# One fused attention and mixture-of-experts kernel: a new instruction order, a sigmoid from silu, and a router with stationary weights

## The chip, the cores and the metric

The kernel runs on one core of a Trainium2 chip, as one program that is launched once. The metric is the device time of one execution in microseconds (us). The engines are named as in the profile: PE (TensorE's matmuls) and PEld (its weight loads), DVE (VectorE), ACT (ScalarE), POOL (GpSimd) and SP (SyncE, which issues most DMAs).

## What is computed

The input x is 8 x 2048 rows of 256 numbers, all float32. A layer norm, linear attention and a residual come first; then a second layer norm, a mixture of experts with a router, a causal convolution of four taps along the sequence, and a second residual:

```python
x = x + attn(layernorm(x))          # Q, K, V of width 64; energy = K^T V over each sequence
x = x + ffn(layernorm(x))
# ffn, with h the normalized rows:
scores = sigmoid(h @ Wr)                       # 8 scores a row
idx = top_k(scores + router_bias, 2)           # two of them are kept
w = scores[idx] / (sum(scores[idx]) + 1e-9)    # cw: these weights, zero elsewhere
hid = silu(h @ Wg[e]) * (h @ Wu[e])            # four experts of width 128
out = sum_e cw[e] * (hid @ Wd[e]) + (cw[4] + cw[6]) * h + cw[7] * relu(h) + conv(h) + conv_b
```

## The kernel before, in words

The 16384 rows are cut into 32 groups of 512 (four tiles of 128 rows); four groups make one sequence. The work on a group is cut into stages, and the loop is a software pipeline: in one step each stage works on another group (`LAG`, line 34). The stages are L (statistics and first norm), A (its Gram matrix and transposes), Q (queries), B (attention, residual, second norm), R (transposes, router), C (the four experts and the convolution) and Y (last part of the experts, output). All steps are unrolled from step 7 to 39 (`steps`, line 319); the first seven are written out in `head()`. Once per sequence a chain of small matmuls turns the Gram matrix into the attention's map, in the step where B is on the first group of the sequence (`st.chain()`, line 91): the chain step, every fourth. `st.drain()` (line 94) is true at the end, when stage A has nothing left.

There is no planner in the code: each engine has a function `body(st)` that lists its part of one step in a fixed order, and semaphores hold an instruction until its input is there. An engine runs its list strictly in order, so that a waiting instruction holds back all behind it.

Products are made of float32r halves: of a number, `hi` is its rounded float32r copy and `lo` the rest, and a product is hi x hi + hi x lo + lo x hi (`three`, line 404). So each tile is copied by ACT to `hi` (for example `hid_high`, line 766), and then the rest is taken by DVE or POOL (`hid_low`, line 1014, `x2T_low`, line 1119, `xn_low`, line 1032, on DVE; `last_low`, line 1329, on POOL for the last expert).

TensorE's order in a step is `body` at line 687: `gate_up(0..7)` (two for each expert e, six matmuls of 512 columns each), `down` (12 matmuls of 256 columns an expert), `x2_transpose`, `router`, `conv_transpose`, the two halves of `attention`, `q_project`, `gram_halves`, `weights_transpose` and `xn_transpose`. `router` (line 537) uses the transposed rows x2T as stationary weights in float32 and 8 columns of Wr as the moving operand, eight matmuls that the profile shows as 16 instructions. `conv_transpose` adds the finished convolution into the experts' PSUM bank and so needs all taps of it.

DVE's order is at line 1225. `conv_tap` (line 1021) adds two of the six convolution taps, one for each half of the columns; `hidden` (line 1004) multiplies up by the weighted gate, `residual`, `norm1_stats` and `norm2_stats` serve the norms, `halo` (line 1162) copies six columns of the group before, and `route` (line 1074) finds the two largest scores and the weights `cw` in some 19 small instructions.

POOL's order is at line 1382: `gate_weight` (line 1322) multiplies an expert's gate by its row weight, 128x512; `power` (line 1366) takes e to the power of minus the logits and adds one, the denominator of the sigmoid; `norm1_factors`, `norm2_factors` and `skip_factors` are instructions on four columns; `relu_add` issues a DMA that adds.

ACT's order is at line 930: `silu` of the gates, the `hi` copies, `logits_copy` (line 865), the norms, `conv_begin`, and the two parts that take skip and relu into the sum.

The sigmoid of the kernel before and the instruction that divides:

```python
g.tensor_tensor(enx[:, :], inv_e[:, :], logits[:, :], ALU.pow)    # POOL, line 1368
g.tensor_tensor(den[:, :], enx[:, :], one_e[:, :], ALU.add)       # POOL, line 1372
v.reciprocal(flat(score[:, :, :]), den[:, :])                     # DVE, line 1088
```

## Time and profile before

| what | value |
|---|---|
| median of 3 runs | 894.48 us (891.71 to 897.38) |
| the profiled execution's own time | 893.6 us |
| its span, first to last instruction | 891.8 us |
| PE busy | 855.9 us, 96% |
| PEld busy | 754.3 us, 85% |
| DVE busy | 741.1 us, 83% |
| ACT busy | 628.7 us, 71% |
| POOL busy | 572.7 us, 64% |
| mean granted TensorE clock | 0.989 of 2.4 GHz |

The profile is of one execution; 1.8 us of its time lie outside the span. Shares are averages over the head, 27 full steps and the drain. Matmuls are pipelined: an instruction's duration overlaps the next one's, and the distance between two starts is what one costs. The same holds for DVE and ACT, where the next instruction's record begins some 0.1 us before the last one ends.

### The profile page before, as it was taken

To read this page: it belongs to the slowest core of one execution; us is meant where nothing else is said; L and a number is where in the kernel's file an instruction comes from. 1 tells how busy PE (TensorE), PEld (TensorE's weight loads), DVE (VectorE), ACT (ScalarE), POOL (GpSimd) and SP (SyncE) were. 2 spreads that over 40 slices of the span, in tenths; PEclk is the share of its full clock that TensorE was granted. 3 is DMA by queue.
4 is the path that set the end of the run, shared out by engine and by line. 5 is a ranking of instruction groups with operands and counts; after the bars stand their busy time and mean duration, and the time that the engine had idled before them with its cause. 6 is when DMAs were issued, how large, how long until landed. Compare 5 with 4: busy or idle time off the path is not lost.

```text
span 891.8 us, 16729 instructions
## 1 busy us (share of the span) xinstructions
PE 855.9 (96%) x5437; PEld 754.3 (85%) x5437; DVE 741.1 (83%) x2056; ACT 628.7 (71%) x1238; POOL 572.7 (64%) x654
## 2 busy tenths in 40 slices
PE   5789999999999999999999999999999999999997
PEld 4668989898888888988889888888888898788876
DVE  5758889988888998888898888899888887767775
ACT  5676777777687777778677777777777775655643
POOL 3336776667676657667666767666576766556663
PEclk9989999999999999999999999999999999999999
DMA  9111434543334543343544343454424344433333
GB/s 286 57 52 47 137 121 142 143 117 99 95 119 142 144 142 68 114 129 120 143 143 114 101 115 99 143 144 142 119 72 119 101 114 119 111 104 100 106 91 84
DMA packets 79446, 103.86 MB, mean 116 GB/s; under 512 B 6528, under 2 KB 58880, under 8 KB 79360
## 3 DMA queue, kind: packets, MB, share of 16 engines
q1 hardware_dynamic: 74752, 86.02, 30.4%
q0 software_dynamic: 4608, 16.78, 10.0%
q8 instruction: 43, 0.70, 0.3%
q14 instruction: 43, 0.35, 0.1%
HBM read 68.96 MB, written 17.04 MB: 96 GB/s over the span
## 4 chain that ended last, share of the span: by engine, by line
PE 66%; DVE 13%; POOL 12%; issue 5%; ACT 4%; DMA 0%; POOLq 0%; ACTq 0%; DVEq 0%
PE ps_gu L406 9%; PE ps_gu L408 9%; PE ps_gu L407 9%; POOL enx L1368 7%; PE ps_y L406 5%; PE ps_y L408 5%; PE ps_y L407 5%; PE ps_sh L543 4%; PE ps_sh L533 3%; POOL gate L1327 3%; PE ps_sh L516 2%; DVE stats L1065 2%; DVE acc L1057 2%; ACT x L840 2%; PE ps_y L456 2%
## 5 line engine op out<-in xcount | busy, mean ns | idle before, releaser
L1327 POOL TENSOR_TENSOR gate<-gate,cwb 128x512 f32<-128x512 f32 x128 | 167.5, 1309 | 127.8 <-ACT gate L763 126.4
L406 PE MATMUL ps_gu<-x2T_hi,wgu_hi 128*128 128x512 f32 x512 | 212.2, 414 | 0.0
L408 PE MATMUL ps_gu<-x2T_hi,wgu_lo 128*128 128x512 f32 x512 | 203.0, 396 | 0.0
L407 PE MATMUL ps_gu<-x2T_lo,wgu_hi 128*128 128x512 f32 x512 | 202.2, 395 | 0.0
L1368 POOL TENSOR_TENSOR enx<-inv_e,logits 128x32 f32<-128x32 f32 x32 | 177.5, 5546 | 8.6 <-ACT logits L756 8.6
L406 PE MATMUL ps_y<-wd_hi,hid_hi 128*128 128x256 f32 x512 | 152.8, 299 | 4.0 <-DVE hid_lo L1018 3.1
L1029 DVE SCALAR_TENSOR_TENSOR conv<-x2T,conv_w,conv 128x512 f32<-128x512 f32 x192 | 146.4, 801 | 0.0
L408 PE MATMUL ps_y<-wd_hi,hid_lo 128*128 128x256 f32 x512 | 145.3, 284 | 0.0
L407 PE MATMUL ps_y<-wd_lo,hid_hi 128*128 128x256 f32 x512 | 144.2, 282 | 0.0
L1011 DVE TENSOR_TENSOR hid<-ps_gu,gate 128x512 f32<-128x512 f32 x128 | 86.0, 672 | 39.2 <-POOL gate L1327 38.1
L408 PEld LDWEIGHTS ps_gu<-x2T_hi,wgu_lo 128*128 128x128 f32 x512 | 96.9, 189 | 22.5
L406 PEld LDWEIGHTS ps_gu<-x2T_hi,wgu_hi 128*128 128x128 f32 x512 | 97.6, 191 | 19.2 <-DVE hid L1011 3.0
L407 PEld LDWEIGHTS ps_gu<-x2T_lo,wgu_hi 128*128 128x128 f32 x512 | 97.4, 190 | 13.4
L406 PEld LDWEIGHTS ps_y<-wd_hi,hid_hi 128*128 128x128 f32 x512 | 98.5, 192 | 6.7 <-DVE hid_lo L1018 4.3
L763 ACT ACTIVATE gate<-ps_gu 128x512 f32<-128x512 f32 x128 | 75.3, 588 | 40.6 <-PE ps_gu L408 39.0
L1018 DVE TENSOR_TENSOR hid_lo<-hid,hid_hi 128x512 fp32r<-128x512 f32 x96 | 68.8, 716 | 41.6 <-ACT hid_hi L756 41.6
L756 ACT ACTIVATE hid_hi<-hid 128x512 fp32r<-128x512 f32 x128 | 80.2, 626 | 32.1 <-DVE hid L1011 31.5
L407 PEld LDWEIGHTS ps_y<-wd_lo,hid_hi 128*128 128x128 f32 x512 | 97.4, 190 | 1.6
L1306 POOL TENSOR_TENSOR mv<-mv,eps_ln 128x4 f32<-128x4 f32 x64 | 13.5, 211 | 132.2 <-DVE mv L1068 112.8
L408 PEld LDWEIGHTS ps_y<-wd_hi,hid_lo 128*128 128x128 f32 x512 | 97.1, 190 | 0.0
L840 ACT ACTIVATE x<-acc,shift,rstd 128x256 f32<-128x256 f32 x128 | 66.5, 591 | 8.8 <-POOL shift L1311 8.2
L824 ACT ACTIVATE xn<-xa,shift,rstd 128x256 f32<-128x256 f32 x128 | 66.0, 589 | 8.2 <-POOL shift L1311 8.1
(115 smaller groups left out, 1934.3 us busy)
## 6 DMA issues: line engine op xcount, KB each, us to landing
cwb<-cw_rows SPq DMA_DIRECT2D x128, 256.0 KB, 4.0
xa<-in_x SPq DMA_DIRECT2D x32, 512.0 KB, 7.5
acc<-in_x SPq DMA_DIRECT2D x32, 512.0 KB, 6.7
acc<-x POOLq DMA_DIRECT2D x32, 512.0 KB, 4.6
out<-acc SPq DMA_DIRECT2D x64, 256.0 KB, 2.3
cwb<-in_wg SPq DMA_DIRECT2D x4, 128.0 KB, 4.0
cwb<-in_wu SPq DMA_DIRECT2D x4, 128.0 KB, 3.8
cwb<-in_wd SPq DMA_DIRECT2D x1, 512.0 KB, 4.5
```

What stands on the lines that cost most here:

```text
L406: nc.tensor.matmul(dst, a_hi, b_hi, start=start, stop=False, skip_group_check=True)
L407: nc.tensor.matmul(dst, a_hi, b_lo, start=False, stop=False, skip_group_check=True)
L408: return nc.tensor.matmul(dst, a_lo, b_hi, start=False, stop=stop, skip_group_check=True)
L756: return nc.scalar.activation(dst, src, ACT.Copy, scale=scale)
L763: nc.scalar.activation(gate[:, e % 2], ps_gu[GU_BANK[2 * e]][:, :], ACT.Silu)\
L824: nc.scalar.activation(xn[:, q, t], xa[:, q, t], ACT.Identity, bias=shift1[:, f, t:t + 1], scale=rstd1[:, f, t:t + 1]).then_inc(xn_ready, 1)
L840: nc.scalar.activation(x2[:, q, t], acc[:, st.slot("B", 4), t], ACT.Identity, bias=shift2[:, q, t:t + 1], scale=rstd2[:, q, t:t + 1]).then ...
L1011: v.tensor_tensor(hid[:, e % 2], ps_gu[GU_BANK[2 * e + 1]][:, :], gate[:, e % 2], ALU.mult)\
L1018: v.tensor_tensor(hid_lo[:, k], hid[:, k], hid_hi[:, k].bitcast(F32), ALU.subtract)\
L1029: v.scalar_tensor_tensor(conv[:, c], x2T[:, q, c, k:k + GT], conv_w[:, c, k:k + 1], conv[:, c], ALU.mult, ALU.add).then_inc(conv_ready, 1)
L1327: g.tensor_tensor(gate[:, e % 2], gate[:, e % 2], cwb[:, q, e], ALU.mult).then_inc(gatew_ready, 1)
L1368: g.tensor_tensor(enx[:, :], inv_e[:, :], logits[:, :], ALU.pow).then_inc(enx_ready, 1)
```

## The change

On TensorE the router becomes four passes of 512 columns: `wr2` holds the hi half of Wr in columns 0 to 7, the lo half in 8 to 15 and zeros beyond, stays as weights, and the hi and lo halves of x2T move through. The result lies transposed, 16 rows by 512; ACT copies it (`logitsT_copy`), and behind the fourth gate-up `logits_rows` transposes it back, four times 16x128. ACT copies the rows (`parts_copy`), and POOL adds the two halves (`logits_sum`).

The sigmoid is made of silu: ACT takes the absolute value (`logits_size`), DVE bounds it from below (`magnitude`), ACT takes silu of its negative (`score_dip`); at the head of `route` DVE divides by the size, adds one where the logit is positive, and takes the larger of the result and its negative. `power` goes.

`xn_low` and the `lo` halves of experts 1 and 2 go from DVE to POOL (`xn_low`, `gate_low`). The order of the four engines changes as the diff shows. Left out of the diff are declarations, the head's and the weights' small additions, and the constants.

```diff
             def router(st):
-                pe.wait_ge(x2T_ready, st.before("R", HC, HC))
+                if st.before("R") == 0:
+                    pe.wait_ge(wrlo_out, 1)
+                b, q = ps_sh[0], st.slot("R", 2)
                 pe.wait_ge(x2Tlo_ready, st.before("R", HC, 1))
-                b, q = ps_sh[0], st.slot("R", 2)
+                pe.wait_ge(x2Thi_ready, st.before("R", HC, HC))
+                for c in range(HC):
+                    nc.tensor.matmul(b[:, :], wr2[:, c], x2T_hi[:, q, c], start=(c == 0), stop=False,
+                                     skip_group_check=True)
+                for c in range(HC):
+                    if c == 1:
+                        pe.wait_ge(x2Tlo_ready, st.before("R", HC, HC))
+                    last = nc.tensor.matmul(b[:, :], wr2[:, c], x2T_lo[:, q, c], start=False, stop=(c == HC - 1),
+                                            skip_group_check=True)
+                last.then_inc(router_done, 1)
+
+            def logits_rows(st):
+                pe.wait_ge(logitsT_ready, st.before("R", 1, 1))
                 for t in range(TG):
-                    for c in range(HC):
-                        last = nc.tensor.matmul(b[:, t * NE:(t + 1) * NE],
-                                                x2T[:, q, c, PAD + t * P:PAD + (t + 1) * P], wr_sb[:, c],
-                                                start=(c == 0), stop=(c == HC - 1))
-                last.then_inc(router_done, 1)
+                    last = nc.tensor.transpose(ps_sh[0][:, t * 2 * NE:(t + 1) * 2 * NE],
+                                               logitsT[0:2 * NE, t * P:(t + 1) * P], ident[0:2 * NE, 0:2 * NE])
+                last.then_inc(rows_done, 1)
...
@@ -711,24 +734,22 @@
                     pe.wait_ge(et_out, st.chains(2, 2))
                 if c_on:
                     gate_up(st, 3)
+                if r_on:
+                    logits_rows(st)
                 if m_on:
                     chain_f(st)
-                if b_on and drain:
+                elif b_on:
                     attention(st, 0)
                 if c_on:
                     gate_up(st, 4)
-                if b_on and drain:
+                if b_on and not m_on:
                     attention(st, 1)
                 if c_on:
+                    gate_up(st, 5)
                     conv_transpose(st)
                     down(st, "C", 0)
-                if b_on and not m_on and not drain:
-                    attention(st, 0)
-                if c_on:
-                    gate_up(st, 5)
                 if m_on:
                     attention(st, 0)
-                if b_on and not drain:
                     attention(st, 1)
                 if c_on:
                     gate_up(st, 6)
...
-            def logits_copy(st):
+            def logitsT_copy(st):
                 act.wait_ge(router_done, st.before("R", 1, 1))
-
+                copy(logitsT[:, :], ps_sh[0][0:2 * NE, :]).then_inc(logitsT_ready, 1)
+
+            def parts_copy(st):
+                act.wait_ge(rows_done, st.before("R", 1, 1))
                 if st.later("R", 1):
-                    act.wait_ge(enx_ready, st.before("R"))
-                copy(logits[:, :], ps_sh[0][:, 0:TG * NE]).then_inc(logits_ready, 1)
+                    act.wait_ge(logits_ready, st.before("R"))
+                copy(parts[:, :, :], ps_sh[0][:, 0:TG * 2 * NE].rearrange("p (t n) -> p t n", t=TG))\
+                    .then_inc(parts_ready, 1)
+
+            def logits_size(st):
+                act.wait_ge(logits_ready, st.before("R", 1, 1))
+                nc.scalar.activation(size[:, :], logits[:, :], ACT.Abs).then_inc(size_ready, 1)
+
+            def score_dip(st):
+
+                act.wait_ge(mag_ready, st.before("R", 1, 1))
+                if st.later("R", 1):
+                    act.wait_ge(cw_ready, st.before("R"))
+                nc.scalar.activation(dip[:, :], mag[:, :], ACT.Silu, scale=-1.0).then_inc(dip_ready, 1)
...
             def body(st):
                 c_on, r_on, m_on = st.on("C"), st.on("R"), st.chain()
                 if m_on:
                     gram_copy(st)
                 if c_on:
                     silu(st, 0)
+                if st.on("A"):
+                    xn_split(st)
                 if r_on:
                     x2T_out(st, 0)
                 if m_on:
                     gramT_copy(st)
+                elif c_on:
+                    hid_high(st, 0)
                 if r_on:
                     x2T_out(st, 1)
                 if m_on:
@@ -945,27 +1005,26 @@
                     silu(st, 1)
                 if m_on:
                     et_copy(st)
-                if r_on:
-                    logits_copy(st)
+                    hid_high(st, 0)
+                if r_on:
+                    logitsT_copy(st)
+                if c_on and not m_on:
+                    relu_part(st)
+                if r_on:
+                    parts_copy(st)
                 if m_on:
                     f_copy(st)
-                if c_on:
-                    hid_high(st, 0)
-                if st.on("A"):
-                    xn_split(st)
+                    relu_part(st)
+                if c_on:
+                    hid_high(st, 1)
+                if r_on:
+                    logits_size(st)
                 if c_on:
                     silu(st, 2)
-                    hid_high(st, 1)
-
-                    q = st.slot("C", 2)
-                    act.wait_ge(skip_ready, st.before("C", 2, 2))
-                    for t in range(TG):
-                        a = acc[:, st.slot("C", 4), t]
-                        nc.scalar.activation(a, a, ACT.Identity, bias=skip_bias[:, q, t:t + 1],
-                                             scale=skip_scale[:, q, t:t + 1]).then_inc(ident_added, 1)
-                    for t in range(TG):
-                        nc.scalar.activation(x2[:, q, t], x2[:, q, t], ACT.Relu, scale=cw[:, q, EM + 3, t:t + 1])\
-                            .then_inc(relu_ready, 1)
+                if r_on:
+                    score_dip(st)
+                if c_on:
+                    skip_part(st)
                 if r_on:
                     conv_begin(st)
                 if c_on:
@@ -973,10 +1032,10 @@
                     hid_high(st, 2)
                 if st.on("L"):
                     norm1(st)
+                if st.on("B") and not m_on:
+                    norm2(st)
                 if r_on:
                     weights_copy(st)
-                if st.on("B") and st.drain():
-                    norm2(st)
                 if st.on("Q"):
                     q_high(st)
                 if st.on("A") and r_on:
@@ -985,7 +1044,7 @@
                     hid_high(st, 3)
                 if st.on("A") and r_on:
                     xnT_high(st, 1)
-                if st.on("B") and not st.drain():
+                if m_on:
                     norm2(st)
...
-            def xn_low(st):
-                dve.wait_ge(xnhi_ready, halved(st, 1))
-
-                dve.wait_ge(gram_done, st.before("A"))
-                v.tensor_tensor(xn_lo, xn[:, st.slot("A", 4)], xn_hi.bitcast(F32), ALU.subtract)\
-                    .then_inc(xnlo_ready, 1)
...
+            def magnitude(st):
+                dve.wait_ge(size_ready, st.before("R", 1, 1))
+                if st.later("R", 1):
+                    dve.wait_ge(dip_ready, st.before("R"))
+                v.tensor_scalar(mag[:, :], size[:, :], LEAST, None, ALU.max).then_inc(mag_ready, 1)
...
-                dve.wait_ge(den_ready, st.before("R", 1, 1))
-                done(v.reciprocal(flat(score[:, :, :]), den[:, :]))
+                dve.wait_ge(mag_ready, st.before("R", 1, 1))
+                done(v.reciprocal(rmag[:, :], mag[:, :]))
+                dve.wait_ge(dip_ready, st.before("R", 1, 1))
+                after()
+                done(v.tensor_tensor(minor[:, :], dip[:, :], rmag[:, :], ALU.mult))
+                after()
+                done(v.scalar_tensor_tensor(signed[:, :], logits[:, :], 0.0, minor[:, :], ALU.is_gt, ALU.add))
+                after()
+                done(v.scalar_tensor_tensor(flat(score[:, :, :]), signed[:, :], -1.0, signed[:, :], ALU.mult, ALU.max))
...
@@ -1229,43 +1298,37 @@
                 if c_on:
                     dve.wait_ge(halo_ready, st.before("C", 1, 1))
                     conv_tap(st, 0)
+                    hidden(st, 0)
+                if r_on:
+                    x2T_low(st, 0)
+                if c_on:
+                    conv_tap(st, 1)
+                if r_on:
+                    x2T_low(st, 1)
                 if st.on("L"):
                     norm1_stats(st)
-                if r_on:
-                    x2T_low(st, 0)
-                if c_on:
-                    conv_tap(st, 1)
-                if r_on:
-                    x2T_low(st, 1)
+                if c_on:
+                    hid_low(st, 0)
+                if c_on:
+                    hidden(st, 1)
                 if y_on:
                     output(st, 0)
                     output(st, 1)
-                if c_on:
-                    hidden(st, 0)
+                if r_on:
+                    magnitude(st)
+                if c_on:
                     conv_tap(st, 2)
-                    hid_low(st, 0)
-                    hidden(st, 1)
-
                 if m_on:
                     f_low(st)
-                drain = st.drain()
-                if c_on:
-                    hid_low(st, 1)
-                if st.on("A"):
-                    xn_low(st)
-                if b_on and drain:
+                elif b_on:
                     residual(st, 0)
                     residual(st, 1)
                     norm2_stats(st)
-                if r_on and c_on and not b_on:
+                if c_on:
+                    hidden(st, 2)
+                if r_on:
                     route(st)
-                if c_on:
-                    hidden(st, 2)
-                if r_on and c_on and b_on:
-                    route(st)
-                if c_on:
-                    hid_low(st, 2)
-                if b_on and not drain:
+                if m_on:
                     residual(st, 0)
                     residual(st, 1)
                     norm2_stats(st)
...
+            def gate_low(st, e):
+
+                pool.wait_ge(hidhi_ready, st.before("C", EM, e + 1))
+                k = e % 2
+                g.tensor_tensor(hid_lo[:, k], hid[:, k], hid_hi[:, k].bitcast(F32), ALU.subtract)\
+                    .then_inc(hidlo_ready[k], 1)
+
+            def xn_low(st):
+                pool.wait_ge(xnhi_ready, halved(st, 1))
+                g.tensor_tensor(xn_lo, xn[:, st.slot("A", 4)], xn_hi.bitcast(F32), ALU.subtract)\
+                    .then_inc(xnlo_ready, 1)
...
-            def power(st):
-                pool.wait_ge(logits_ready, st.before("R", 1, 1))
-                g.tensor_tensor(enx[:, :], inv_e[:, :], logits[:, :], ALU.pow).then_inc(enx_ready, 1)
-                pool.wait_ge(enx_ready, st.before("R", 1, 1))
+            def logits_sum(st):
+                pool.wait_ge(parts_ready, st.before("R", 1, 1))
                 if st.later("R", 1):
-                    pool.wait_ge(rt, st.before("R", RT, 1 - RT))
-                g.tensor_tensor(den[:, :], enx[:, :], one_e[:, :], ALU.add).then_inc(den_ready, 1)
+                    pool.wait_ge(cw_ready, st.before("R"))
+                    pool.wait_ge(size_ready, st.before("R"))
+                g.tensor_tensor(logits[:, :].rearrange("p (t e) -> p t e", t=TG), parts[:, :, 0:NE],
+                                parts[:, :, NE:2 * NE], ALU.add).then_inc(logits_ready, 1)
...
             def body(st):
-                c_on, r_on = st.on("C"), st.on("R")
+                c_on, r_on, b_on, m_on = st.on("C"), st.on("R"), st.on("B"), st.chain()
                 if c_on:
                     gate_weight(st, 0)
+                if st.on("A"):
+                    xn_low(st)
+                if c_on:
                     gate_weight(st, 1)
-                if r_on:
-                    power(st)
-                if c_on:
+                norm1_factors(st)
+                if r_on:
+                    logits_sum(st)
+                if c_on:
+                    gate_low(st, 1)
                     gate_weight(st, 2)
-                    norm1_factors(st)
-                    if st.drain():
-                        relu_add(st)
-                        if st.on("B"):
-                            norm2_factors(st)
+                if b_on and not m_on:
+                    norm2_factors(st)
+                if c_on:
+                    gate_low(st, 2)
                     gate_weight(st, 3)
-                if c_on and not st.drain():
                     relu_add(st)
-                if st.on("B") and not st.drain():
+                if m_on:
                     norm2_factors(st)
                 if c_on:
-                    last_low(st)
+                    gate_low(st, 3)
                 if r_on:
                     skip_factors(st)
```

## Rows read from the trace of the kernel before

**Rows 1.** Busy us by stretch: PE, PEld, DVE, ACT, POOL (instructions); clock, DMA share, GB/s.
```profile
167.21:192.50 25.29, 25.29 (x168) 22.61 (x166) 22.67 (x65) 19.19 (x39) 17.63 (x21) 1.00 0.44 126
...
217.90:246.60 28.70, 28.66 (x189) 24.87 (x187) 24.23 (x66) 20.97 (x46) 18.71 (x21) 1.00 0.40 111
...
sum 104.79, PE 104.64 PEld 92.81 DVE 92.64 ACT 78.65 POOL 71.85; mean PE 26.16 PEld 23.20 DVE 23.16 ACT 19.66 POOL 17.96
```

**Rows 2.** Timeline of PE in an ordinary step: start, us, engine, line, operation, shape, count.
```profile
167.21 0.48 PE L406 MATMUL ps_gu<-x2T_hi,wgu_hi 128*128 128x512 f32 x1
...
172.06 0.60 PE L533 MATMUL ps_sh<-ident,x 128*128 128x128 f32 x4
172.41 0.48 PE L406 MATMUL ps_gu<-x2T_hi,wgu_hi 128*128 128x512 f32 x1
172.73 0.39 PE L407 MATMUL ps_gu<-x2T_lo,wgu_hi 128*128 128x512 f32 x1
...
173.89 1.85 PE L543 MATMUL ps_sh<-wr_sb,x2T 128*128 128x8 f32 x16
175.59 0.47 PE L406 MATMUL ps_gu<-x2T_hi,wgu_hi 128*128 128x512 f32 x1
```

**Rows 3.** Timeline of DVE, four stretches.
```profile
67.74 2.41 DVE L1029 SCALAR_TENSOR_TENSOR conv<-x2T,conv_w,conv 128x512 f32<-128x512 f32 x2
...
122.96 2.26 DVE L1029 SCALAR_TENSOR_TENSOR conv<-x2T,conv_w,conv 128x512 f32<-128x512 f32 x2
...
168.87 0.71 DVE L1172 COPY x2T<-x2T 128x6 f32<-128x6 f32 x1
169.49 1.42 DVE L1029 SCALAR_TENSOR_TENSOR conv<-x2T,conv_w,conv 128x512 f32<-128x512 f32 x2
170.83 1.40 DVE L1046 BATCH_NORM_STATS2 stats<-xa 128x6 f32<-128x256 f32 x4
...
172.62 0.65 DVE L1122 TENSOR_TENSOR x2T_lo<-ps_sh,x2T_hi 128x512 fp32r<-128x512 f32 x1
...
180.81 1.22 DVE L1036 TENSOR_TENSOR xnT<-xn,xnT 128x1024 fp32r<-128x1024 f32 x1
...
186.04 1.08 DVE L1101 SCALAR_TENSOR_TENSOR raw<-marked,score 128x32 f32<-128x32 f32 x1
```

**Rows 4.** Timeline of POOL in the same stretches.
```profile
67.73 1.87 POOL L1327 TENSOR_TENSOR gate<-gate,cwb 128x512 f32<-128x512 f32 x1 [1.12 <-ACT gate L763]
...
122.74 1.27 POOL L1327 TENSOR_TENSOR gate<-gate,cwb 128x512 f32<-128x512 f32 x1 [3.88 <-ACT gate L763]
...
168.25 1.30 POOL L1332 TENSOR_TENSOR hid_lo<-hid,hid_hi 128x512 fp32r<-128x512 f32 x1
...
171.07 1.29 POOL L1327 TENSOR_TENSOR gate<-gate,cwb 128x512 f32<-128x512 f32 x1
...
176.06 5.44 POOL L1368 TENSOR_TENSOR enx<-inv_e,logits 128x32 f32<-128x32 f32 x1
...
185.78 1.30 POOL L1327 TENSOR_TENSOR gate<-gate,cwb 128x512 f32<-128x512 f32 x1 [0.69 <-ACT gate L763]
```

**Rows 5.** Timeline of ACT just ahead of an ordinary step.
```profile
167.12 0.62 ACT L756 ACTIVATE hid_hi<-hid 128x512 fp32r<-128x512 f32 x1
```

**Rows 6.** Groups of POOL: line, operation, shapes, count, busy us, mean ns, idle before.
```profile
L1368 POOL TENSOR_TENSOR enx<-inv_e,logits 128x32 f32<-128x32 f32 x32 | 177.5, 5546 | 8.6 <-ACT logits L756 8.6
L1327 POOL TENSOR_TENSOR gate<-gate,cwb 128x512 f32<-128x512 f32 x128 | 167.5, 1309 | 127.8 <-ACT gate L763 126.4 <-DMA cwb<-cw_rows 1.4
...
L1306 POOL TENSOR_TENSOR mv<-mv,eps_ln 128x4 f32<-128x4 f32 x64 | 13.5, 211 | 132.2 <-DVE mv L1068 112.8 <-DVE mv L1049 18.6 <-ACT xn L824 0.8
```

**Rows 7.** Groups of ACT, the same columns.
```profile
L967 ACT ACTIVATE x<-x,cw 128x256 f32<-128x256 f32 x128 | 54.2, 495 | 0.0
...
L763 ACT ACT_TABLE_LOAD x1 | 1.3, 1283 | 0.0
```

**Rows 8.** Waits of PE's weight loads: total us, times, longest us.
```profile
PEld ps_sh L606 <- DVE cw L1115: 6.0, 4, 1.8
```

74 lines of the change are left out of this document (51 added, 23 removed).

## The prediction

> **What bounds the kernel now.** I first read the busy time by stretch, cut where a step's first gate-up matmul starts [rows 1]. An ordinary step (167.21 to 192.50) takes 25.3 us and TensorE is busy in all of it at full clock; every fourth, the chain step, takes 28.7 with 28.66 busy. DVE has 22.7 of 25.3, ACT 19.2, POOL 17.6. So a step is TensorE's instructions laid end to end, and one of another engine costs nothing until a matmul waits for it. Second, TensorE's order within one step [rows 2]: which matmul starts when tells how late each input may be. Third, DVE and POOL side by side [rows 3, 4]: where the small slack of the others goes. Four steps take 104.8 us; the loop has 27 full steps (7 of them chain steps) and a drain of six.
>
> **The pair of engines that cannot overlap.** At 122.74 a POOL product (1.27 us) begins; the two convolution taps that DVE starts at 122.96 take 2.26 instead of the 1.42 of the pair at 169.49. At 186.04 a 128x32 instruction of DVE takes 1.08 and ends 0.04 after the POOL product of 185.78; at 168.87 a copy of six columns takes 0.71 and ends with POOL's hid_lo. The other way round: at 67.73 the taps were first, and POOL's product took 1.87. DVE instructions with one input in SBUF (batch statistics at 170.83 beside POOL's product of 171.07: 1.40 for four, 0.41 each) run beside POOL undisturbed, and so does xn_low beside the long pow, at 180.81 beside 176.06: pow is long but does not hold what DVE needs [rows 3, 4]. So a large POOL instruction and a DVE instruction with two SBUF inputs exclude each other: the later one waits for the other's end, a tap then ends some 0.55 after it, and in the pair of taps POOL gets its turn between them. The change takes the harmless 5.4 us of pow off POOL and puts four excluding instructions there.
>
> **The parts, and their cost.**
> *Router.* Out go 16 instructions from 173.89 to 175.59, 1.70, plus the longer first pitch behind small matmuls, 0.08 (172.41 to 172.73 is 0.32, not 0.23): 1.78. In come four passes of 512 columns at 0.23 (the five matmuls from 172.73 to 173.89): 0.92. The four row transposes, with 16 rows and 16 moving columns, are not in the trace. The nearest row is the four 128x128 transposes, 0.35 at 172.06 plus 0.08 behind: 0.11 each, and the router's sixteen come to 0.11 each too, which is the upper end; below, 16 moving columns instead of 128 could make them nearly free, 0.03 each. I take the nearest row, 0.11, so 0.43 together. Gain 1.78 - 0.92 - 0.43 = 0.43 a step, up to 0.74. "TensorE: Matmul & The Clock Gate" (the Trainium skill, LDWEIGHTS) says that a weight load costs by its columns (number / 1.2 in ns) and not by its rows. By that rule 128 columns are 0.107 and the four transposes 0.43, an estimate, where the lower bound would make them 0.12; no row here shows a load of 16 rows.
> *Sigmoid.* POOL loses pow, 5.5 a step [rows 6], and a small addition; ACT gains two small activations, a rows copy and a 16x512 copy instead of a small one, about 1.1; DVE gains magnitude, minor, signed and a max, about 0.2 each. All of it is off TensorE's path as long as its users are not late: rows wait for the copy of the transposed logits (0.2 after the router, 0.6 long, against 1.39 of gate-up cover), the second attention half for the rows copy (cover 1.9).
> *xn_low to POOL.* DVE loses 1.22. On POOL a 128x1024 subtraction is not in the trace: at least the 1.31 of the 128x512 product, at most twice it, 2.62. From 0.21 at 4 elements and 1.31 at 512 a line gives 2.4; I take that [rows 6].
> *hid_low 1 and 2 to POOL.* DVE loses 2 x 0.6, POOL gains 2 x 1.3. POOL's excluding work goes from 5 x 1.3 to 7 x 1.3 + 2.4 = 11.5 of 25 us.
> *Order.* attention halves, the convolution transposes and ACT's and POOL's parts move; what counts is who is late now. DMA issues stay in their queues.
>
> **First wait, in an ordinary step.** Times from the start of gate-up 0 (167.21), by hand from the rows. ACT's hid_high 3 starts 0.09 before it and takes 0.62 [rows 5], so POOL's gate_low 3 runs 0.57 to 1.86, the halo copy ends with it and the skip factors alternate with conv tap 0. Gate product 0 came 2.82 after that hid_lo (168.25 to 171.07), so 3.39 to 4.68. Only then comes hidden 0 (4.72 to 5.39) and x2T_low 0 (to 5.99). xn_low has the pair from 4.64 to 7.03; conv tap 1, asking at 5.92, ends 7.58 and 8.25 instead of 6.66 and 7.34; x2T_low 1 ends 8.84. The router's fourth pass needs it. In TensorE's order the router starts at 6.68 and this pass at 7.37: wait 1.5. Before, the router needed no second half of x2T_lo. Behind xn_low on POOL stands gate product 1, which hidden 1 has not asked for yet. Bounds: with xn_low at 1.3 the taps run unhindered, x2T_low 1 ends 7.94 and the wait is 0.6; at 2.62 it is 1.7.
>
> **Second wait.** Router done 9.1; then gate-up 3, rows, attention 0, gate-up 4, attention 1, gate-up 5: the convolution transposes are due at 14.64. DVE after x2T_low 1: statistics 1.8 (170.83 to 172.62), hid_low 0.6, hidden 1 0.6 (11.8), two outputs 1.2: 13.0, then magnitude. But hidden 1 lets ACT copy (to 12.49) and POOL start gate_low 1, 12.5 to 13.8. Magnitude waits until 13.85; gate product 2, its gate ready at 13.6, is in front of conv tap 2 until 15.0; the taps end at 15.55 and 16.2. Wait 1.6. If the taps come first, the product falls between them and the end is the same to 0.1; with both taps ahead of it, about 0.6. Ordinary step: 25.3 - 0.43 + 1.5 + 1.6 = 28.0.
>
> **Chain step.** The router is later behind the chain matmuls, so the first wait is gone. But magnitude stands ahead of conv tap 2 on DVE and waits for ACT's logits_size, which now stands behind f_copy (from 12.1, 0.7), four relu parts (0.5 each, 0.1 of it beneath the next, [rows 7]) and hid_high 1: 15.2. By then gate_low 1 holds the pair to 16.4 and gate product 2 to 17.6; taps end 18.8; transposes due at 14.9: wait 3.9. 28.7 - 0.43 + 3.9 = 32.2. Behind it norm2 stands at ACT's end as before, and x2's first transposes wait 0.3: 28.4. Route, norm2 statistics, gate_low 2 and weights end over 0.7 before their users in both.
>
> **Sum.** Four steps 2 x 28.0 + 32.2 + 28.4 = 116.6 against 104.8: +11.8. 26 full steps (the last has no xn_low) are 6.5 of these: +77. Head and drain, where TensorE is not the bound and pow goes but the exclusion stays: 0, between -8 and +5. The profiled execution took 893.6 (span 891.8), 0.9 under the median of the runs, 894.48: 893.6 + 77 = about **970**.
>
> **Rivals.**
> *The gain arrives whole* (faster; place: POOL's meetings with DVE). pow, 5.5 us, stands between the logits and the weights of every group, and in the drain the transposes of the weights wait up to 1.8 for them [rows 6, 8]. If POOL's new products fall beside DVE instructions that read PSUM or one operand, as nearly all do now (the pair of taps at 169.49 is undisturbed), no wait is added: 0.43 in each of 31 steps with a router is 13, and 1.7 in six drain steps about 10: 893.6 - 23 = **870**. More it cannot be in the full steps: a chain step has 0.04 of TensorE idle. Against it: by the walk above POOL takes the pair while taps 1 and 2 are next on DVE. It decides where the added waits average under 0.43 a step.
> *DVE gets its turn whenever it asks.* For it: at 67.73 taps that began 0.01 after the product were served first. Against it: 122.96, 168.87, 186.04 and some 25 like it. Then x2T_low 1 ends near 7.8 (wait 0.45, step 25.3), the second wait vanishes, the chain step still waits 1.75 for logits_size (30.0): four steps 105.9, 26 of them +7, the drain -10: **891**.
> *Half of it collides*: xn_low takes 1.3 and both taps of conv 2 come ahead of gate product 2. Waits 0.6 and 0.6, steps 26.1, 31.2 and 26.4: four 109.8, +33, **927**: same side, smaller.
> *Activation tables swap.* If Abs and Silu were in different tables, each step would load twice, 1.28 each [rows 7]; before, there are two loads in the whole run. logits_size, then silu 2 come 1.3 later, and with them the second wait: +1.3 x 26 on the forecast, **1004**. "ScalarE: Activation LUTs" (the Trainium skill, Table sets) says that cheap functions, abs among them, are in every set; by that this cannot happen. No row has Abs, so I keep a small chance.
>
> **How the numbers follow.** Forecast 0.72, with its own range 935 to 1000; half collision 0.09; gain whole 0.10; DVE first 0.05; tables 0.04. A change of 1% (885.5 to 903.4) is about what a measurement of this kernel tells from none: DVE first lies within it, with 0.01 of the whole gain; a little of it goes below. So faster 0.11, same 0.06, slower 0.83. Range 890 to 1003: the whole gain, half of DVE first and the tables stay outside.
>
> **What would show it.** Right: ordinary steps of about 28 us; a TensorE gap of 1 to 2 us ahead of the router's last pass, released by DVE's x2T_lo, and one ahead of the convolution transposes, released by conv; taps of 1.3 to 1.8 us beside POOL's xn_low and gate; POOL's xn_low near 2.4; sixteen router instructions of 1.7 us replaced by 0.9 + 0.43. Wrong: TensorE still without gaps and a step under 25.3; taps all at 0.74; POOL products of 1.8 us instead, which would be DVE first; table loads in every step.

## The result, and the profile after

The changed kernel takes 1121.5 us (median of 4 runs, 1119.8 to 1124.9), the kernel before 894.6 in the same comparison: ratio 1.254, interval 1.250 to 1.257. The forecast was 970, its range 890 to 1003. The side was right; the size was short by 151 us. The profiled execution spans 1121.1 us.

The table of stretches, the full steps and then the drain, first of after, then of before; the columns are those of [rows 1].

```profile
58.96:934.16 875.20, 731.80 (x4204) 618.40 (x4203) 618.57 (x1692) 535.33 (x1084) 451.61 (x567) 0.93 0.33 92
934.16:1121.10 186.94, 146.65 (x780) 120.26 (x778) 108.97 (x274) 85.49 (x180) 75.65 (x94) 0.91 0.29 82
```

```profile
56.88:742.17 685.29, 680.41 (x4413) 603.26 (x4411) 601.06 (x1664) 511.45 (x1006) 463.23 (x514) 1.00 0.41 118
742.17:891.80 149.63, 136.10 (x820) 117.19 (x818) 104.74 (x266) 82.61 (x168) 88.25 (x89) 0.98 0.36 103
```

Of the 229 us between the spans, 190 came in the 27 full steps, 37 in the drain, 2 in the head (58.96 instead of 56.88). In the steps TensorE was busy in 680 of 685 us; now it is in 732 of 875, and the granted clock fell from 1.00 to 0.93. So PE has gaps, and no other engine is busy for a larger share of the steps than before: the time is in waits. One ordinary step, the chain step, and the sum of four steps (from 300.35 on):

```profile
333.05:365.84 32.79, 27.97 (x159) 23.55 (x158) 23.11 (x66) 20.04 (x41) 17.19 (x22) 0.92 0.34 97
...
398.73:433.58 34.85, 31.15 (x181) 26.61 (x179) 24.65 (x67) 21.23 (x46) 17.36 (x22) 0.90 0.32 92
sum 133.23, PE 113.67 PEld 96.09 DVE 93.98 ACT 82.50 POOL 70.01; mean PE 28.42 PEld 24.02 DVE 23.49 ACT 20.63 POOL 17.50
```

The steps were forecast at 28.0, 32.2 (chain) and 28.4 (behind it), 116.6 for four; they are 133.2. The waits of after (engine, tile, line waited for: us in total, times, longest), PE's and one of ACT's:

```profile
PE ps_y L467 <- DVE conv L1088: 64.0, 30, 5.0
PE ps_sh L527 <- ACT cwT L777: 63.1, 20, 3.8
PE ps_sh L555 <- ACT x2T_hi L777: 23.0, 15, 3.2
PE ps_sh L560 <- DVE x2T_lo L1187: 12.2, 16, 0.8
...
ACT x L863 <- issue: 129.9, 23, 7.8
```

Lines 467 and 560 are the two waits that were forecast, the convolution transposes and the router's last passes; line 555 is the router's first passes. Line 527, the second half of xn's transposes, waits for ACT's copy of the weights; nothing of it was in the forecast. And ACT itself stands 5.6 us in each of 23 steps (129.9 / 23) ahead of line 863, norm2, "issue", that is, for nothing that the profile names. The timeline of one ordinary step shows for what (start, us, engine, line, [idle before]):

```profile
358.31 0.92 POOL L1408 DMA_DIRECT2D acc<-x  x1
...
362.94 2.07 ACT L863 ACTIVATE x<-acc,shift,rstd 128x256 f32<-128x256 f32 x4 [5.22 <-issue]
364.92 0.25 ACT L777 ACTIVATE cwT<-ps_sh 16x128 f32<-16x128 f32 x1
...
365.31 0.88 PE L527 MATMUL ps_sh<-ident,xn 128*128 128x128 f32 x4 [3.09 <-ACT cwT L777]
...
333.63 0.63 PE L418 MATMUL ps_gu<-x2T_lo,wgu_hi 128*128 128x512 f32 x1
334.05 0.63 PE L419 MATMUL ps_gu<-x2T_hi,wgu_lo 128*128 128x512 f32 x1
```

The stretch from there on, its granted clock the last but two, and the DMA in the list of issues (KB each, us from issue to landing):

```profile
333.63:337.89 4.26, 4.26 (x11) 3.29 (x10) 2.90 (x5) 2.85 (x5) 3.27 (x6) 0.50 0.62 206
```

```profile
acc<-x POOLq DMA_DIRECT2D x32, 512.0 KB, 4.6
```

POOL issues `relu_add`'s accumulating DMA at 358.31. It lands 4.6 us later, at 362.9; norm2 starts at 362.94. In the steps on either side it is the same: issued at 325.24 and 391.33, norm2 at 329.94 and 395.98. norm2 writes x2, in two buffers; the one that it needs is the one this DMA is still reading, that of the group two before. The wait is in the code, `act.wait_ge(relu_added[...])` in `norm2`, and it was there before. What the change did is to move norm2 ahead of the weights copy in ordinary steps, so that the copy and all behind it on ACT stand behind the DMA. Then TensorE, after more than 3 us without work, starts the next step late and at nearly twice the distance from matmul to matmul: 0.42 us (333.63 to 334.05) instead of 0.23 [rows 2], with a granted clock of 0.50, the lower of its levels (1.2 of 2.4 GHz), until 337.89. In the kernel before, the DMA and norm2 of the step of 167.21:

```profile
187.03 0.92 POOL L1340 DMA_DIRECT2D acc<-x  x1
...
193.73 2.08 ACT L840 ACTIVATE x<-acc,shift,rstd 128x256 f32<-128x256 f32 x4 [0.18 <-POOL shift L1311]
```

With the same 4.6 us the DMA landed at 191.6, before ACT came to norm2, its last part, at 193.7.

The two forecast waits, in the steps from 300.35 and 333.05:

```profile
305.96 2.37 POOL L1400 TENSOR_TENSOR xnT<-xn,xnT 128x1024 fp32r<-128x1024 f32 x1
...
307.24 2.30 DVE L1088 SCALAR_TENSOR_TENSOR conv<-x2T,conv_w,conv 128x512 f32<-128x512 f32 x2
...
309.46 0.68 DVE L1187 TENSOR_TENSOR x2T_lo<-ps_sh,x2T_hi 128x512 fp32r<-128x512 f32 x1
...
310.19 0.51 PE L560 MATMUL ps_sh<-x2T_lo,wr 128*128 128x512 f32 x1 [0.75 <-DVE x2T_lo L1187]
...
346.89 1.29 POOL L1395 TENSOR_TENSOR hid_lo<-hid,hid_hi 128x512 fp32r<-128x512 f32 x1
...
347.23 0.99 DVE L1130 TENSOR_SCALAR mag<-size 128x32 f32<-128x32 f32 x1 [0.32 <-ACT size L901]
...
348.13 1.29 POOL L1389 TENSOR_TENSOR gate<-gate,cwb 128x512 f32<-128x512 f32 x1
348.13 2.50 DVE L1088 SCALAR_TENSOR_TENSOR conv<-x2T,conv_w,conv 128x512 f32<-128x512 f32 x2
350.69 0.55 PE L467 MATMUL ps_y<-ident,conv 128*128 128x128 f32 x3 [1.74 <-DVE conv L1088]
```

They are as forecast: taps 1 wait for the end of xn_low (308.33) and take 2.30, x2T_low 1 comes behind them; magnitude ends with gate_low 1 (348.2), taps 2 with 1.1 us under gate product 2. Three groups of after: xn_low takes 2.38 (2.4 was taken), magnitude 1.02 on average, and of the two table loads in the whole run one stands at the first silu of the scores, so nothing swaps in the steps.

```profile
L1400 POOL TENSOR_TENSOR xnT<-xn,xnT 128x1024 fp32r<-128x1024 f32 x26 | 61.9, 2382 | 0.0
L1130 DVE TENSOR_SCALAR mag<-size 128x32 f32<-128x32 f32 x32 | 32.6, 1020 | 22.1 <-ACT size L901 22.1
...
L908 ACT ACT_TABLE_LOAD x1 | 1.3, 1283 | 0.0
```

### The profile page after: what moved, and what is told of

The parts are those of the page before. It is cut to its first block and busy times, and to the rows that moved or that the text cites. A ratio compares the mean times of both kernels' runs of the same rounds, so it can differ in the third digit from the quotient of the medians.

```text
span 1121.1 us, 16479 instructions
## 1 busy us (share of the span) xinstructions
PE 918.0 (82%) x5181; PEld 771.5 (69%) x5181; DVE 763.1 (68%) x2095; ACT 657.7 (59%) x1335; POOL 543.6 (48%) x711
## 5 line engine op out<-in xcount | busy, mean ns | idle before, releaser
L1395 POOL TENSOR_TENSOR hid_lo<-hid,hid_hi 128x512 fp32r<-128x512 f32 x96 | 123.9, 1290 | 306.7 <-ACT hid_hi L777 306.7
L417 PE MATMUL ps_gu<-x2T_hi,wgu_hi 128*128 128x512 f32 x512 | 223.5, 436 | 0.4 <-DVE hid L1070 0.4
L418 PE MATMUL ps_gu<-x2T_lo,wgu_hi 128*128 128x512 f32 x512 | 216.0, 422 | 0.0
L419 PE MATMUL ps_gu<-x2T_hi,wgu_lo 128*128 128x512 f32 x512 | 214.9, 420 | 0.0
L1088 DVE SCALAR_TENSOR_TENSOR conv<-x2T,conv_w,conv 128x512 f32<-128x512 f32 x192 | 188.2, 1019 | 0.0
L863 ACT ACTIVATE x<-acc,shift,rstd 128x256 f32<-128x256 f32 x128 | 66.4, 590 | 135.5 <-issue 129.9
L419 PEld LDWEIGHTS ps_gu<-x2T_hi,wgu_lo 128*128 128x128 f32 x512 | 105.4, 206 | 25.6
L417 PEld LDWEIGHTS ps_gu<-x2T_hi,wgu_hi 128*128 128x128 f32 x512 | 106.5, 208 | 19.3 <-DVE hid L1070 3.1
L1200 DVE TENSOR_TENSOR q<-ps_gu,q 64x512 fp32r<-64x512 f32 x32 | 21.8, 682 | 135.0 <-ACT q L777 135.0
L527 PE MATMUL ps_sh<-ident,xn 128*128 128x128 f32 x256 | 45.4, 313 | 76.0 <-ACT cwT L777 63.1
L1368 POOL TENSOR_TENSOR mv<-mv,eps_ln 128x4 f32<-128x4 f32 x64 | 22.9, 358 | 141.6 <-DVE mv L1120 98.8
```

Source lines behind the costliest of these rows:

```text
L417: nc.tensor.matmul(dst, a_hi, b_hi, start=start, stop=False, skip_group_check=True)
L418: nc.tensor.matmul(dst, a_hi, b_lo, start=False, stop=False, skip_group_check=True)
L419: return nc.tensor.matmul(dst, a_lo, b_hi, start=False, stop=stop, skip_group_check=True)
L527: last = nc.tensor.transpose(ps_sh[c][:, t * P:(t + 1) * P], xn[:, st.slot("A", 4), t, c * P:(c + 1) * P], ident[:, :])
L863: nc.scalar.activation(x2[:, q, t], acc[:, st.slot("B", 4), t], ACT.Identity, bias=shift2[:, q, t:t + 1], scale=rstd2[:, q, t:t + 1]).then ...
L1088: v.scalar_tensor_tensor(conv[:, c], x2T[:, q, c, k:k + GT], conv_w[:, c, k:k + 1], conv[:, c], ALU.mult, ALU.add).then_inc(conv_ready, 1)
```

## The experiments

Each is one run beside the kernel before (890 to 897 us); e14 and e15 have three more rounds. "Four steps" is the sum of one chain step and three ordinary ones.

**1. norm2 back at ACT's end** (e1), as before, outside the drain; in the drain it stays where the change put it.

```diff
-                if st.on("B") and not m_on:
+                if st.on("B") and st.drain():
                     norm2(st)
...
-                if m_on:
+                if st.on("B") and not st.drain():
                     norm2(st)
```

> Theory A (norm2, moved ahead of the weights copy on ACT, waits for the DMA of relu_add; the second half of xn's transposes then comes 3.3 us late and the matmuls behind it run at half clock, together 5.9 us in three of four steps): with norm2 back at ACT's end four steps fall from 133.2 to about 115.5 and the time to 990-1020. Theory B (POOL and DVE excluding each other is the whole of it, norm2's wait only stands beside it): the step stays near 33 us, time above 1100.

1046.9 us, four steps 122.4. The wait of line 527 for the weights copy is gone, theory B falls. The gain is less than theory A gave (990 to 1020). norm2, 2 us at ACT's end, now stands ahead of the next step's copies of x2T, and line 555 waits 38.1 us for x2T_hi in all, where it was 23.0; that this is the whole difference was not shown. The drain is as long as in the changed kernel, 186.9.

**2. The DMA earlier, norm2 where the change put it** (e2).

```diff
                     gate_low(st, 1)
                     gate_weight(st, 2)
+                    relu_add(st)
...
                     gate_weight(st, 3)
-                    relu_add(st)
```

> norm2 keeps its new place, but its DMA is issued ahead of gate_low 2 and gate product 3 and lands before norm2 asks. Theory A: as with norm2 at the end, four steps about 115.5, and the drain gains too: 980-1015. Theory B: above 1100. Theory C (norm2 ahead of the weights copy is late by its own factors and 2 us long, the DMA has no part in it): 1060 or more.

1005.2 us: one line moved on POOL is worth 116 us, 97.8 in the full steps (777.4 instead of 875.2) and 19.6 in the drain (167.3 instead of 186.9). An ordinary step and the chain step behind it, and lines of the first's timeline:

```profile
332.85:361.38 28.53, 25.53 (x160) 21.71 (x159) 24.01 (x65) 20.21 (x42) 17.76 (x22) 1.00 0.38 111
361.38:395.46 34.08, 30.38 (x181) 26.34 (x179) 23.75 (x66) 20.16 (x45) 17.26 (x22) 0.90 0.34 94
```

```profile
349.70 0.93 POOL L1408 DMA_DIRECT2D acc<-x  x1 [1.31 <-ACT acc L976]
...
354.63 2.07 ACT L847 ACTIVATE xn<-xa,shift,rstd 128x256 f32<-128x256 f32 x4
356.60 2.07 ACT L863 ACTIVATE x<-acc,shift,rstd 128x256 f32<-128x256 f32 x4
359.36 0.27 ACT L777 ACTIVATE cwT<-ps_sh 16x128 f32<-16x128 f32 x1 [0.69 <-PE ps_sh L629]
```

The DMA is issued 6.9 us ahead of norm2, which follows norm1 without a gap, and the copy waits for nothing but its transposes. Theory A holds, though four steps take 119.8 and not its 115.5; theory C falls, since the copy no longer waits for norm2 once norm2's buffer is free. And the steps that are left, 28.5, 34.1 and 28.7 (395.46 to 424.15), come near the forecast ones: 28.0, 32.2 and 28.4.

**3. Gap or clock** (e12). In the changed kernel, 13 matmuls that nobody reads fill the gap ahead of line 527, the wait kept.

```diff
+                    if c_on and b_on and not m_on:
+                        pe.wait_ge(gate_ready, st.before("C", EM, EM))
+                        for _ in range(13):
+                            nc.tensor.matmul(ps_gu[GU_BANK[0]][:, :], wgu_hi[:, 0, 0, 0], x2T_hi[:, st.slot("C", 2), 0],
+                                             start=True, stop=True)
                     xn_transpose(st, 1)
```

> The changed kernel itself (1121.5 us), with 13 extra matmuls of 512 columns (3.0 us, their result is overwritten) in the gap ahead of the second half of xn's transposes, in the steps in which norm2 stands early. The wait stays. If a gap costs its length and then a clock at half speed behind it (12 matmuls at 0.43 instead of 0.23 us): the pitch behind stays 0.23 and four steps fall by about 4.5, time near 1090. If the matmuls behind the gap are slow for another reason: still 0.43, 1121 or more. If the next waits of the step end no sooner anyway: pitch 0.23, but 1115-1121.

```profile
363.56 0.63 PE L527 MATMUL ps_sh<-ident,xn 128*128 128x128 f32 x4
...
364.26 0.39 PE L418 MATMUL ps_gu<-x2T_lo,wgu_hi 128*128 128x512 f32 x1
364.49 0.40 PE L419 MATMUL ps_gu<-x2T_hi,wgu_lo 128*128 128x512 f32 x1
```

```profile
PE ps_sh L555 <- ACT x2T_hi L782: 42.9, 24, 3.2
```

The distance behind the filled gap is 0.23, so the idle time did lower the clock; yet the time is 1123.0, within what the changed kernel itself took (1119.8 to 1124.9), so the third branch. What the matmuls gained waits again one line on: line 555 for x2T_hi 42.9 us in all (23.0 without filling). The next step is late on ACT, and TensorE's half speed stood beside that. The 116 us are the held-up ACT, not the clock behind this gap.

**4. POOL's long products cut short** (e7), the order of e2 kept; parts of the two lo halves are left out.

```diff
-                g.tensor_tensor(hid_lo[:, k], hid[:, k], hid_hi[:, k].bitcast(F32), ALU.subtract)\
+                n = 16 if e == 1 and st.later("C", 2) else GT
+                g.tensor_tensor(hid_lo[:, k, 0:n], hid[:, k, 0:n], hid_hi[:, k, 0:n].bitcast(F32), ALU.subtract)\
...
-                g.tensor_tensor(xn_lo, xn[:, st.slot("A", 4)], xn_hi.bitcast(F32), ALU.subtract)\
+                g.tensor_tensor(xn_lo[:, 0:1, 0:16], xn[:, st.slot("A", 4), 0:1, 0:16],
+                                xn_hi[:, 0:1, 0:16].bitcast(F32), ALU.subtract)\
```

> The order of e2 untouched; POOL's xn_low takes 16 columns instead of 1024 and gate_low 1 takes 16 instead of 512, so the rest of both lo halves is left out of the result. If POOL's long products hold DVE's taps: taps 1 run at 0.74, the router's wait falls from 0.9 to 0.3 or less, the wait of the convolution transposes from 2.1 to about 1 (gate product 2 still meets a tap), four steps about 114, 965-985 us. If DVE's and ACT's order alone makes the waits: 1000-1006.

950.2 us, better than expected; four steps take 112.5. Line 560 no longer waits, line 467 waits 37.8 in all instead of 67.3. So shortening them is worth 55 of the 111 us that e2 is over the kernel before. How much of that is the exclusion and how much POOL's own shorter list, the run doesn't part, except at line 560, where xn_low can act through DVE alone. Line 555 still waits 20.4 us for x2T_hi (18.7 in e2), which the forecast did not have: the change put hid_high 0, which waits for DVE's hidden 0, ahead of x2T_out 1 on ACT. In e13 (experiment 8), where among other moves it stands behind, this wait is 1.8 us. The chain step is still 32.1; most of its wait is another, for ACT's logits_size.

**5. Tap 2 ahead of magnitude** (e9), on e2.

```diff
-                if r_on:
-                    magnitude(st)
                 if c_on:
                     conv_tap(st, 2)
+                if r_on:
+                    magnitude(st)
```

> e2 (1005.2 us) with conv tap 2 ahead of magnitude on DVE and nothing else. If what holds the convolution transposes is magnitude, which waits for logits_sum behind norm1_factors on POOL, and in the chain step for ACT's logits_size: the chain step's wait falls from 5 to about 1 us, the ordinary one's from 2.1 to 1 (one tap still meets gate_low 1), four steps from 119.0 to 111-113, 955-970 us. If the taps meet POOL's products whichever comes first: 990 or more.

953.0 us, four steps 108.6, the chain step 27.8 instead of 34.1 and so under the 28.7 of the kernel before. The convolution transposes wait 12.0 us in all instead of 67.3. What POOL's products delay here is small as long as tap 2 does not stand behind magnitude. Experiments 4 and 5 act on the same wait, so their gains can't simply be added; no run has both.

The 6.3 us of the chain step are more than its wait. In e2:

```profile
380.43 1.97 PE L467 MATMUL ps_y<-ident,conv 128*128 128x128 f32 x8 [3.66 <-DVE conv L1088]
382.05 0.56 PE L417 MATMUL ps_y<-wd_hi,hid_hi 128*128 128x256 f32 x1
```

```profile
382.05:384.75 2.70, 2.70 (x14) 2.70 (x13) 2.39 (x22) 1.52 (x2) 0.00 (x0) 0.50 0.97 184
387.48:388.90 1.42, 1.42 (x13) 1.42 (x12) 1.39 (x9) 1.23 (x3) 0.02 (x1) 1.00 0.00 0
```

The matmul before starts at 376.37, so the wait, less one distance of 0.23, is 3.8. Behind it the granted clock is 0.50: the twelve matmuls of down 0 take 2.70, those of down 1, at 1.00, 1.42. From 380.43 to the next gate-up at 386.08 TensorE takes 5.65, where the same work takes 3.3 in the one full chain step of e2 that kept its clock (from 500.13). So the wait and 2.3 us of half clock make nearly all of the 6.3. In five of the six full chain steps with this wait the clock costs 1.5 to 2.3 us, some 9 us together.

**6. xn_low on DVE again** (e3), on e2, behind hidden 0.

```diff
                     hidden(st, 0)
+                if st.on("A"):
+                    xn_low(st)
...
-                if st.on("A"):
-                    xn_low(st)
```

> As the run before, with xn_low back on DVE, behind hidden 0. If what is left after the norm2 wait is the exclusion between DVE and POOL, as the prediction had it, the router's wait (up to 1.5 us a step) goes and the time is 30-40 us under the run before. If xn_low's place has no part in what is left: within 10 us of the run before.

1039.3 us, 34 worse: a miss. Now x2T_low stands 1.2 us behind xn_low on DVE, the taps 1 are under gate product 1 instead of xn_low (the pair still takes 2.44 in the step from 344.99, where e2 has 2.33), and line 560 waits 39.8 instead of 14.9. The exclusion takes the next product that comes.

**7. x2T_low 1 ahead of tap 1** (e5), on e2, and tap 2 ahead of hid_low 0 as well (e6).

> relu_add early as in e2 (1005.2 us, four steps 119.0), and on DVE both x2T_low ahead of conv tap 1. If the router's wait comes from x2T_low 1 standing behind taps that POOL's xn_low holds up: that wait (0.9 us in three of four steps, with what the clock loses behind it) goes, four steps about 116, 980-990 us. If the wait ahead of the convolution transposes takes it back (its chain through norm1_factors and logits_sum on POOL does not start earlier): within 5 us of 1005.

> As e5, and conv tap 2 ahead of hid_low 0 and hidden 1, so that it no longer stands behind magnitude. If magnitude and POOL's gate_low 1 and gate product 2 make the second wait: it goes in all steps (2.1 in ordinary ones, 5 in chain steps), four steps 104-107, and 11 us of the drain: 900-930. If the exclusion only moves (the taps meet gate product 1 instead, hidden 1 and what follows it come later): 960 or more.

e5: 1074.0 us, worse by 69, against all that was expected. The router's wait for x2T_lo is gone, but DVE stands 1.07 us for x2T_hi 1, both taps then meet gate product 1, norm1's statistics come later, POOL's norm1_factors behind them, logits_sum behind these, and so magnitude and tap 2: line 467 waits 117.3 us in all. That chain through POOL is a part of the second wait which the forecast did not have; no run moved it alone. e6: 961.5, the chain step 27.8, but line 467 still waits in ordinary steps (28.0 to 28.4), now for the outputs that stand behind tap 2 (DVE's acc: 36.6 us in 21 steps).

**8. The waits taken out one after the other** (e13, e14, e15), on e9. Below is e13 on DVE; norm1_factors on POOL goes behind gate product 2, and in ordinary steps hid_high 0 on ACT behind x2T_out 1. e14 puts x2T_low 1 ahead of the two outputs, e15 moves route and norm2 in the drain:

```diff
+                if y_on:
+                    output(st, 0)
+                    output(st, 1)
                 if r_on:
                     x2T_low(st, 1)
                 if c_on:
                     conv_tap(st, 1)
-                if st.on("L"):
-                    norm1_stats(st)
...
+                    conv_tap(st, 2)
+                    hid_low(st, 0)
+                    hidden(st, 1)
+                if st.on("L"):
+                    norm1_stats(st)
```

> e9 (953.0 us, four steps 108.6) with what then is left taken out: on DVE both outputs between the two x2T_low, taps 1 and 2 together behind them and the statistics of norm1 behind hidden 1; on ACT hid_high 0 behind x2T_out 1; on POOL logits_sum ahead of norm1_factors. If the router's two waits (0.9 us each in ordinary steps) are all that is left: four steps 104-105.5, 923-935 us. If DVE itself, with 23 to 24 us of work a step and the exclusion on top, sets the step by then: 107 or more, 945 or more.

> e13 (918.2 us, four steps 106.2) with both x2T_low side by side and the outputs behind them. What is left in its ordinary steps is one wait of the router's fourth pass, 0.95 us, for x2T_low 1 behind the two outputs. If that is the last one: ordinary steps 25.1-25.3, four steps 103.2-104, 898-905 us, so the full steps are then at or under the 104.8 of the kernel before. If the outputs, now later, push taps 1 and 2 past the convolution transposes: 912 or more.

> As e14, and in the drain route ahead of norm2's statistics on DVE, norm2_factors behind gate product 3 on POOL, norm2 behind the weights copy on ACT. If the drain's loss (some 9 us over the kernel before) is the weights' transposes waiting up to 2.8 us for route, and the weights copy waiting behind norm2: 3 to 8 us less than e14, 892-900. If norm2, then later, makes the next x2 transposes wait instead: within 2 us of e14.

e13: 918.2 us, four steps 106.2, the steps longer than expected and the whole shorter. e14: 920.5 (ratio 1.030, 1.026 to 1.035), a miss: the router's last wait is gone, and another has come in its place, at the transposes of the weights (e13: 6.5 us, 4 times).

```profile
PE ps_sh L629 <- DVE cw L1180: 29.9, 24, 3.5
```

Four steps take 106.0, as with e13. The wait has moved along DVE's list from an early user to its last one, route. That points to DVE's list, with what holds it, as what sets the step by then; no run showed it by itself. e15: 925.5 (ratio 1.035, 1.027 to 1.043); the drain's rest was not the late route, or norm2 took it back; it stays open.

**9. The new parts in the old order** (e4; e8 and e10 move x2T_low 1 ahead; e11 the drain). Router, sigmoid and their helpers, with the order of the kernel before on all engines, xn_low and hid_low 1 and 2 on DVE; magnitude behind hid_low 1, score_dip behind the relu parts (e8 has both ahead).

> The new router and the new sigmoid alone, everything else in the order of the kernel before (halves of hid and xn on DVE again). By the prediction's own terms: 0.43 to 0.74 in each of 31 steps and about 10 in the drain, 865-885. If one of the new parts costs by itself (the transposes of 16 rows, a clock drop behind them, the two waits that rows and their copies add), 895 or more.

> As e4 (913.6 us: new router and sigmoid in the old order), with x2T_low 1 ahead of conv tap 1, magnitude ahead of hid_low 1 and score_dip ahead of the skip and relu parts. If what cost there was the router's fourth pass waiting for x2T_low 1 (0.5 to 0.7 a step) and the weights' transposes in the drain waiting 1.5 longer for the longer chain of the new sigmoid: 888-897 us. If the new parts cost by themselves: 908 or more.

> e4 (913.6 us, four steps 105.4) with x2T_low 1 between the two halves of conv tap 1 instead of behind both: 0.66 us earlier, and no new wait, since its input is there by then. If the router's fourth pass waits for it by 0.5 to 0.6 in ordinary steps: four steps 103.3-103.9, 899-904 us. If the e8 run's loss (an earlier x2T_low pushes tap 1 under POOL's gate product) comes here too: 920 or more.

> As e10, and in the drain alone magnitude ahead of hid_low 1, score_dip ahead of skip and relu, route ahead of norm2's statistics and hidden 2. If the drain's 11 us over the kernel before are the weights' transposes waiting for a route that stands late on DVE: 2 to 2.5 us less in four of its steps, 889-895 us. If norm2, then later, takes it back: within 2 us of e10.

e4: 913.6 us, against 865 to 885 if the parts had paid as forecast. e8, both x2T_low ahead of conv tap 1: 951.7, a miss of e5's kind (tap 1 under gate product 1; line 417 waits 41.4 us for hid on DVE; ordinary steps 27.0 to 29.0). e10, x2T_low 1 between the halves of tap 1: 904.1, the router without a wait in the full steps, ordinary steps 25.5 to 25.7, so four steps 105.1 and not the 103.3 to 103.9 expected. e11: 905.1; the drain's wait moved from the weights' transposes to the down product, which waits 10.4 us for hid_lo. So the new parts without the new order are not faster either. Their price on TensorE, where nothing is late (the step of e14 at 469):

```profile
469.16 0.40 PE L419 MATMUL ps_gu<-x2T_hi,wgu_lo 128*128 128x512 f32 x1
469.43 0.70 PE L555 MATMUL ps_sh<-x2T_hi,wr 128*128 128x512 f32 x2
...
470.43 0.39 PE L417 MATMUL ps_gu<-x2T_hi,wgu_hi 128*128 128x512 f32 x1
...
471.58 0.39 PE L419 MATMUL ps_gu<-x2T_hi,wgu_lo 128*128 128x512 f32 x1
471.90 0.42 PE L567 MATMUL ps_sh<-ident,logitsT 16*128 16x16 f32 x4
472.24 0.39 PE L615 MATMUL ps_sh<-f,q 128*128 128x256 f32 x1
472.46 0.28 PE L616 MATMUL ps_sh<-f,q 128*128 128x256 f32 x1
```

The four passes take 1.00 (469.43 to 470.43), and the distance ahead of them is 0.04 longer; the four transposes take 0.34, with 0.09 ahead (471.58 to 471.90 is 0.32) and 0.10 behind (0.22, not 0.12). That is 1.57 in place of 1.78.

## Why the prediction was wrong

**The step that failed** is the sentence "Route, norm2 statistics, gate_low 2 and weights end over 0.7 before their users in both", with "DMA issues stay in their queues" under *Order*. The weights do not end 0.7 before their user: line 527 waits up to 3.8 us for their copy. norm2's statistics were looked at, norm2 itself was not: its wait for the buffer that the DMA of the group two before still reads, and what its new place puts behind that wait on ACT (weights copy, q_high, both xnT_high, hid_high 3). The DMA's issue stayed in its queue; the instruction that waits for it was moved forward in ACT's list to right behind norm1, some 5 us (in before's step norm1 ends at 188.1 and norm2 starts at 193.7). e2 prices it: 116 of the 151 us missing. The half clock behind this gap, seen in the trace, has no part of its own in it (e12). Of the 35 us that e2 is over the forecast, 15 are in the full steps, 18 in the drain, 2 in the head.

**The drain** was put at -8 to +5 and is 37 us longer. 19.6 of it is the same wait (e2). 8 more go with the moves of experiments 5 and 8, which act in the drain too: in e13 it is 159.0 (757.36 to 916.40) instead of 167.3. The last 9.4 over before stay. e4 and e10, with the old order, have 161.0 and 157.1, which points to the new parts: the chain from router to weights is longer by four instructions on DVE and three on ACT, and in the drain TensorE waits for its end. No run showed which of them counts.

**The two forecast waits** were right in place and nearly in size. In e2's steps the distances between starts, less 0.23, give:

```profile
340.08 0.71 PE L555 MATMUL ps_sh<-x2T_hi,wr 128*128 128x512 f32 x2 [0.54 <-ACT x2T_hi L777]
...
341.79 0.50 PE L560 MATMUL ps_sh<-x2T_lo,wr 128*128 128x512 f32 x1 [0.77 <-DVE x2T_lo L1187]
```

First wait: 1.5 forecast, 1.6 measured, 0.7 of it for x2T_hi (339.15 to 340.08) and 0.9 for x2T_lo (340.62 to 341.79). The mechanism, x2T_low 1 behind taps 1 under xn_low, is the forecast one (e7 ends the wait for x2T_lo); the part for x2T_hi was not seen. Second: 1.6 forecast, 1.9 measured (347.55 to 349.64); not seen was that logits_sum stands behind norm1_factors on POOL (e5). With the router's gain as measured, 25.3 - 0.2 + 1.6 + 1.9 = 28.6, and the step takes 28.5. Chain step: 3.9 forecast, 3.8 measured, as forecast behind logits_size (it ends 15.3 us into the step, at 376.71; 15.2 was forecast). The forecast has no term for the clock behind it, up to 2.3 us; that is mainly why this step is 34.1 and not 32.2. Four steps of e2 are 119.8 where 116.6 was forecast; its 27 full steps are 92 us longer than before (777.4 against 685.3), where the forecast had 77 for 26. Some 9 of these 15 us are the clock of the chain steps.

**The router's gain** was mis-sized: 0.43 a step forecast, 0.21 measured (1.78 - 1.57). The passes were taken at 0.23 each, 0.92 in all; they cost 1.04, since the first distance is 0.31 and the one ahead of them 0.04 longer. The row transposes were taken at 0.43 with the distance behind them, and that came out (0.34 and 0.10), but 0.09 ahead of them was not counted. By the Trainium skill, "TensorE: Matmul & The Clock Gate" (LDWEIGHTS), by whose rule a weight load costs by its columns and not by its rows, the four transposes were estimated at 0.43. The trace of e14 agrees that the rows don't count: the weight loads of 16 rows and 128 columns take 0.139 us on average, those of 128 rows for the other transposes 0.141 and 0.148.

**The rivals.** No table swap: Abs brought no load, and there are two loads in the run, as before. DVE is not served first: taps 1 take 2.30 beside xn_low, which takes its 2.37. The prediction's own row for this rival was against it too: the pair at 67.74 took 2.41, not 1.42 [rows 3]. Half collision falls with taps of 2.3 to 2.5 a pair. The gain arriving whole falls with e4 and e10 too: with the old order 0.21 a step is won on TensorE, and in e10 waits of 4.6 us in all for norm2 (3.1 before) and 4.1 for hid stand against it. Its full steps take 687.4 (before 685.3), its drain 157.1 (before 149.6), so these waits are not the whole of it.

## What to carry to other kernels

When a part is moved forward in an engine's list, check every semaphore it waits on, not only its input: a buffer that a DMA still reads counts from the DMA's landing, so from where another engine issues it, and all behind the part waits too. An idle that the profile puts down to "issue" is worth a look at the code's waits. A wait that was taken out is a gain only when the next user in the same list is not as late: measure the step, not the wait (e5, e12, e14). And a long wait of TensorE can cost more than its length, by the clock behind it (the chain step of e2).

## What was not expected of the hardware

magnitude and the copy of the two maxima have one input in SBUF and 8 to 32 columns, and were held like the taps: 1.02 us on average for magnitude and 0.80 for the copy (line 1161), where e4 has 0.17 and 0.27. In the step of e4 from 304.31 no large POOL product runs beside magnitude (318.69).

```profile
L1138 DVE TENSOR_SCALAR mag<-size 128x32 f32<-128x32 f32 x32 | 5.5, 172 | 3.6 <-ACT size L906 3.6
```

Batch statistics and instructions that read PSUM ran beside POOL undisturbed in the steps looked at. So it is not the number of SBUF inputs alone, as the prediction put it; its own row of 168.87, a copy with one input that ended with POOL's product, already said so [rows 3]. And filling a gap on TensorE with unused matmuls kept the distance at 0.23, but was worth nothing in time.
